# The last expert's context loaded behind the first gathered rows, and a new order of VectorE and ScalarE up to the fourth tile

## The chip, the cores and the metric

The kernel runs on one core of a Trainium2 chip. The time is device time in microseconds, the median of three runs: 295.52 us (295.21 to 295.55).

## The reference

The input x has 4 batches of 512 rows of 512 numbers. Two blocks follow each other, each with a layer norm before and a gated residual after.

```
x = x + tanh(g_xattn) * A(layernorm(x))
x = x + tanh(g_ffn)   * F(layernorm(x))
```

A routes each row by its token id to one of 4 experts: `expert = min(clip(id, 0, 24999) // 6250, 3)`. The expert's three matrices are all the same 512x512 matrix, ctx[e]: `g = silu(h @ ctx[e].T)`, `u = h @ ctx[e].T`, `y = (g * u) @ ctx[e].T`. F averages a batch's rows, picks 2 of 6 experts by a softmax, and mixes `gelu(h @ W1 + b1) @ W2 + b2` of both, with 352 hidden units. All is float32.

## The kernel before

The 2048 rows are sorted by expert into 19 tiles of 128 rows (`TILES`, N/128 + E - 1). The first four tiles are the first tile of each expert, so tile j < 4 uses expert j. The routing is computed on the chip: VectorE ranks the token ids, TensorE inverts the ranking with one-hot matrices (`invert`, L960), and VectorE turns the result into row numbers (`rows_of`, L571), first for the tiles 0 to 3 and later, from `tile_hot`, for the rest. GpSimd gathers the rows of a tile by an indirect DMA (L423) into a ring of six places, and scatters the finished ones (L435).

Float32 products are done in three passes of rounded halves: each operand is split into a high part (ScalarE copies from PSUM with rounding) and a low part (VectorE subtracts the high part from PSUM). For a tile j the steps are: `rows_statistics` and `normalise` (VectorE, with an inverse root on GpSimd between), `transpose_h` (TensorE, L974), `h_high` (ScalarE), `h_low` (VectorE), `first_product` (TensorE, 12 matmuls of 512 columns, L1020), `silu_of` (ScalarE), `up` (VectorE), `transpose_a` (L981), `a_high`, `a_low`, `second_product` (L1034), and `residual` (VectorE, L591).

Before it, each ctx[e] is loaded by one DMA of SP's queue (L347), transposed in four pieces n = 4e to 4e+3 (`transpose_ctx(n)`, L1039) into one of four PSUM banks n mod 4, and split: `ctx_high(n)` on ScalarE (L817), `ctx_low(n)` on VectorE (L625). For the pieces in `BY_ACT` (8 and 9) the low part is made otherwise: TensorE transposes again and subtracts the high part with a negated identity (`rest_of_ctx`, L1051), and ScalarE copies the result (`ctx_low_alone`, L821). A bank is free for piece n + 4 when the low part of piece n is done.

Every engine runs a program in an order written out by hand, and waits on semaphores. SP's queue issues the token ids and the four contexts at once, then waits for much later events. VectorE's order up to the third tile is L630 to L665, ScalarE's L831 to L852, TensorE's L1061 to L1091. After them the tiles are done in loops (L666, L853, L1102), the first block's last tiles overlap the start of the second block, and the four batches of the second block follow.

The change touches the constant `BY_ACT`, the loop of L346, and these three hand-written stretches.

Of the kernel before, what the change touches and what calls it, by code (L numbers as in the profile page):

```python
# [51 lines left out]
class Chain:  # L52
# [18 lines left out]
    def run(self, ins, apart=False):  # L71
        self.wait(self.sign(ins), apart)


def flamingo_kernel(nc, x, ids, ctx, g_xattn, g_ffn, gate_w, w1, b1, w2, b2, out):
# [8 lines left out]
    IDC = N // P  # L84
    FIRST_BY_POOL = 3
    FAR = 1024.0
    WARM = (10, 10)
    TILES = N // P + E - 1
    RING = 6
# [3 lines left out]
    EARLY = TT + E - 1  # L93
    PREP = TILES - 7
    LATER = TILES - E
    BY_ACT = (8, 9)
    BY_DVE = tuple(n for n in range(E * KD) if n not in BY_ACT)
    FC = -(-F2 // P)
    FM = [min(P, F2 - c * P) for c in range(FC)]
# [13 lines left out]
    with ExitStack() as stack:  # L113
# [229 lines left out]
        @block.sync  # L343
        def _(sp):
            sp.dma_start(ids_i[:, :], ids.rearrange("b s -> (b s)").rearrange("(p c) -> p c", c=IDC)).then_inc(ids_here, 16)
            for e in range(E):  # L346
                sp.dma_start(raw_ctx[:, e], ctx[e].rearrange("(k p) d -> p k d", p=P)).then_inc(ctx_here[e], 16)  # L347

            for counted in primed:
                sp.sem_inc(counted, 1)  # L350

            def load_x1(b):
                for t in range(TT):
                    sp.dma_start(x1_of(b, t * DS, DS),
                                 x1_rows[bass.ds(b * S + t * P, P), :]).then_inc(x1_here[t], 16)

            def load_experts(b):
                wait_apart(sp, gate_ready, b + 1, waited)
                full = (FC - 1) * P
                chosen = [sp.value_load(top_idx[0:1, s:s + 1], min_val=0, max_val=NE - 1) for s in range(2)]  # L360
                for s, e in enumerate(chosen):
                    if b > 0:
                        sp.wait_ge(lo_done[s], len(PARTS) * b)
                    raw = w_raw[s]
                    for piece, width in ((0, slice(0, P)), (1, slice(P, F2))):
                        sp.dma_start(part_of(raw, piece),
                                     w1[bass.ds(e, 1), :, width].rearrange("o (k p) f -> p (o k) f", p=P)
                                     ).then_inc((w1_here if width.start == 0 else w1_rest_here)[s], 16)
                    sp.dma_start(raw[:, W1N:W1N + (FC - 1) * D].rearrange("p (c d) -> p c d", d=D),
                                 w2[bass.ds(e, 1), 0:full].rearrange("o (c p) d -> p (o c) d", p=P)).then_inc(w2_here[s], 16)  # L370
                    last = raw[:, W1N + (FC - 1) * D:WN]
                    sp.dma_start(last[0:FM[-1], :], w2[bass.ds(e, 1), full:F2].rearrange("o f d -> (o f) d")).then_inc(w2_here[s], 16)
                    sp.dma_start(last[BIAS_ROW:BIAS_ROW + 1, :], b2[bass.ds(e, 1), :]).then_inc(w2_here[s], 16)

            def store(b):
                for t in range(TT):
                    wait_apart(sp, o_taken, TT * b + t + 2, waited)
                    sp.dma_start(out.rearrange("b s d -> (b s) d")[bass.ds(b * S + t * P, P), :],
                                 x1_of(b, t * DS, D)).then_inc(out_stored, 16)

            sp.wait_ge(ctxT_done, E * KD)
            sp.wait_ge(tiles_landed, EARLY)
            load_x1(0)
            sp.wait_ge(rows_done, 1)
            sp.wait_ge(pads_made, 3)
            load_experts(0)
            sp.wait_ge(tiles_landed, TILES)
            for b in range(0, B - 1):
                wait_apart(sp, h2_ready, TT * b + TT, waited)
                wait_apart(sp, out_stored, 16 * TT * b + 1, waited)  # L390
                load_x1(b + 1)
                load_experts(b + 1)
                store(b)
            store(B - 1)
            wait_primed(sp, out_stored, 16 * TT * B)
# [98 lines left out]
        def _(dve):  # L494
# [89 lines left out]
            def rows_statistics(j):  # L584

                dve.wait_ge(gathered[j % RING], 16 * (j // RING) + 16)
                run(dve.bn_stats(stats1[:, :], ring_row(j, 0, D)), apart=True)  # L587
                run(dve.bn_aggr(mv1[:, :], stats1[:, :]))
                dve.tensor_scalar(ve1[:, :], mv1[:, 1:2], EPS, None, ALU.add).then_inc(ve_ready, 1)
# [11 lines left out]
            def normalise(j):  # L601
                dve.wait_ge(rstd_ready, j + 1)
                at_least(dve, hT_done, j)
                dve.tensor_scalar(h[:, :], ring_row(j, 0, D), mv1[:, 0:1], rstd1[:, :],
                                  ALU.subtract, ALU.mult).then_inc(h_ready, 1)
# [19 lines left out]
            def ctx_low(n):  # L625
                dve.wait_ge(ctx_hi_done, n + 1)
                dve.tensor_tensor(ctx_lo[:, n * F1:(n + 1) * F1], o_ps[n % 4][:, :],  # L627
                                  ctx_hi[:, n * F1:(n + 1) * F1].bitcast(FP32), ALU.subtract).then_inc(ctx_lo_done, 1)

            for n in range(0, 7):  # L630
                ctx_low(n)
            rows_statistics(0)
            ctx_low(7)
            normalise(0)
            rows_statistics(1)
            dve.wait_ge(tg_done, 1)
            h_low(0)
            normalise(1)
# [3 lines left out]
            rows_statistics(2)  # L642
            up(0)
            normalise(2)
            ctx_low(12)
            a_low(0)
            h_low(2)
            up(1)
            dve.wait_ge(ptile_made, 1)
            ones_part = tile_hot[:, :, 1, :]  # L650
            run(dve.tensor_tensor(ones_part, col_h[:, E:TILES].unsqueeze(1).to_broadcast([P, IDC, LATER]),
                                  ptile[:, :].unsqueeze(2).to_broadcast([P, IDC, LATER]), ALU.is_equal))
            dve.tensor_tensor(tile_hot[:, :, 0, :], ones_part, token_h[:, :].unsqueeze(2).to_broadcast([P, IDC, LATER]),
                              ALU.mult).then_inc(tile_hot_done, 1)
            rows_statistics(3)
            ctx_low(13)
            dve.wait_ge(ext_made, 1)
            run(dve.tensor_tensor(ended[:, :, :], col[:, E:TILES].unsqueeze(2).to_broadcast([P, LATER, 2 * E]),
                                  ends[:, :].unsqueeze(1).to_broadcast([P, LATER, 2 * E]), ALU.is_ge))
            run(dve.tensor_reduce(te[:, :], ended[:, :, 0:2 * E - 1], AX_X, ALU.add))  # L660
            dve.scalar_tensor_tensor(te_i[:, :], ended[:, :, E - 1], -float(E), te[:, :], ALU.mult, ALU.add).then_inc(te_made, 1)
            ctx_low(14)
            dve.wait_ge(rows_done, 1)
            rows_of(slice(E, TILES), o_ps[0], LATER, routed)
            ctx_low(15)  # L665
            for j in range(2, PREP):  # L666
                a_low(j - 1)
                normalise(j + 1)
                residual(j - 2)
                h_low(j + 1)  # L670
                up(j)
                rows_statistics(j + 2)
# [117 lines left out]
        def _(sc):  # L790
# [37 lines left out]
            sc.wait_ge(tg_done, 1)  # L828
            bring_tables(ACT.Silu)

            for n in range(0, 8):  # L831
                ctx_high(n)
            sc.wait_ge(gwT_done, 1)
            sc.activation(gwT[:, :, :], y_ps[:, 0:KD * NE].rearrange("p (k e) -> p k e", e=NE), ACT.Copy).then_inc(gwT_copied, 1)
            for c in range(FC):
                sc.activation(b1T[0:FM[c], c, :], y_ps[0:FM[c], (KD + c) * NE:(KD + c + 1) * NE], ACT.Copy).then_inc(gwT_copied, 1)
            ctx_high(8)
            ctx_high(9)
            ctx_low_alone(8)
            ctx_high(10)  # L840
            ctx_low_alone(9)
            ctx_high(11)
            h_high(0)
            ctx_high(12)
            h_high(1)
            silu_of(0)
            ctx_high(13)
            a_high(0)
            h_high(2)
            silu_of(1)  # L850
            ctx_high(14)
            ctx_high(15)  # L852
            for j in range(2, PREP):  # L853
                a_high(j - 1)
                silu_of(j)
# [76 lines left out]
        def _(pe):  # L932
# [130 lines left out]
            transpose_ctx(0)  # L1063
            transpose_ctx(1)
            transpose_ctx(2)
            pe.wait_ge(slot_hot_done, IDC)
            pe.wait_ge(first_hot_done, 1)
            invert(aT_ps, slot_hot, first_hot, E).then_inc(first_rows_done, 1)
            for n in range(3, 8):
                transpose_ctx(n)  # L1070
            turn_small_tables()
            transpose_ctx(8)
            transpose_ctx(9)
            rest_of_ctx(8)
            transpose_ctx(10)
            rest_of_ctx(9)
            transpose_ctx(11)

            transpose_h(0)
            transpose_ctx(12)  # L1080
            first_product(0, 0, lambda: transpose_h(1))
            transpose_ctx(13)
            first_product(1, 1)
            transpose_a(0)
            transpose_h(2)
            transpose_ctx(14)
            second_product(0, 0)
            transpose_ctx(15)
            pe.wait_ge(tile_hot_done, 1)
            pe.wait_ge(ctx_lo_done, by_dve_until(13))  # L1090
# [160 lines left out]
```

## Time and profile before

| | |
|---|---|
| median of three runs | 295.52 us |
| profiled execution, its own time | 295.37 us |
| its span | 293.6 us |
| TensorE (PE) busy | 282.3 us, 96% |
| VectorE (DVE) busy | 205.1 us, 70% |
| ScalarE (ACT) busy | 108.9 us, 37% |
| GpSimd (POOL) busy | 70.1 us, 24% |
| granted TensorE clock, mean | 0.999 of full speed |

The span runs from the first to the last recorded instruction; 1.8 us of the execution's own time lie around it. Busy times are those of single instructions; matmuls are pipelined, so starts of successive instructions tell more than their durations. Names such as L996 are lines of the kernel, often those of a helper that serves many calls.

### The profile page before, as it was taken

To read this page: it belongs to the slowest core of one execution; us is meant where nothing else is said; L and a number is where in the kernel's file an instruction comes from. 1 tells how busy PE (TensorE), PEld (TensorE's weight loads), DVE (VectorE), ACT (ScalarE), POOL (GpSimd) and SP (SyncE) were. 2 spreads that over 40 slices of the span, in tenths; PEclk is the share of its full clock that TensorE was granted. 3 is DMA by queue.
4 is the path that set the end of the run, shared out by engine and by line. 5 is a ranking of instruction groups with operands and counts; after the bars stand their busy time and mean duration, and the time that the engine had idled before them with its cause. 6 is when DMAs were issued, how large, how long until landed. Compare 5 with 4: busy or idle time off the path is not lost.

```text
span 293.6 us, 4400 instructions
## 1 busy us (share of the span) xinstructions
PE 282.3 (96%) x1426; PEld 227.5 (78%) x1426; DVE 205.1 (70%) x449; ACT 108.9 (37%) x191; POOL 70.1 (24%) x108
## 2 busy tenths in 40 slices
PE   6879899999999999999999999999999999999995
PEld 6668688888888888867786877877788777878874
DVE  7867978878887898697769455786465854846133
ACT  4655222222223225444254273335443372442010
POOL 4545245555444554442240000000000000000000
PEclk9999999999999999999999999999999999999999
DMA  6930022232245223169115009640576205730003
GB/s 211 393 118 0 14 96 72 72 111 73 75 143 180 74 72 110 36 187 316 73 44 171 2 6 310 224 143 0 165 231 214 74 0 181 214 145 1 0 0 143
DMA packets 21490, 34.44 MB, mean 117 GB/s; under 512 B 1865, under 2 KB 10063, under 8 KB 21469
## 3 DMA queue, kind: packets, MB, share of 16 engines
q1 hardware_dynamic: 18400, 24.16, 25.3%
q0 software_dynamic: 3040, 9.98, 10.2%
q8 instruction: 12, 0.20, 0.3%
q14 instruction: 10, 0.07, 0.1%
q10 hardware_dynamic: 28, 0.02, 0.0%
HBM read 24.97 MB, written 9.19 MB: 116 GB/s over the span
## 4 chain that ended last, share of the span: by engine, by line
PE 84%; DVE 11%; DMA 2%; issue 1%; ACT 1%; POOL 0%; ACTq 0%; POOLq 0%; DVEq 0%
PE bank L996 31%; PE bank L970 15%; PE bank L971 14%; PE bank L972 14%; PE bank L987 3%; PE bank L978 3%; DMA x_ring<-in_x,get_rows 2%; PE bank L1113 2%; DVE x_odd L730 1%; DVE stats L587 1%; DVE ctx_lo L627 1%; PE bank L936 1%; DVE w_lo L710 1%; DVE w_raw L563 1%; DVE aT_lo L616 1%
## 5 line engine op out<-in xcount | busy, mean ns | idle before, releaser
L970 PE MATMUL bank<-w_lo,ctx_hi 128*128 128x512 f32 (+1 forms) x96 | 38.0, 395 | 0.4 <-DVE ctx_lo L723 0.4
L971 PE MATMUL bank<-w_hi,ctx_hi 128*128 128x512 f32 (+1 forms) x96 | 37.5, 391 | 0.0
L972 PE MATMUL bank<-w_hi,ctx_lo 128*128 128x512 f32 (+1 forms) x96 | 37.4, 390 | 0.0
L710 DVE TENSOR_TENSOR w_lo<-w_raw,w_hi 128x512 fp32r<-128x512 f32 (+2 forms) x24 | 27.6, 1172 | 2.6 <-ACT w_hi L874 2.6
L970 PE MATMUL bank<-ctx_lo,w_hi 128*128 128x512 f32 (+1 forms) x72 | 28.6, 397 | 0.0
L971 PE MATMUL bank<-ctx_hi,w_hi 128*128 128x512 f32 (+1 forms) x72 | 28.2, 392 | 0.0
L972 PE MATMUL bank<-ctx_hi,w_lo 128*128 128x512 f32 (+1 forms) x72 | 28.1, 391 | 0.0
L722 DVE TENSOR_SCALAR ctx_hi<-act,mix 128x512 fp32r<-128x512 f32 x16 | 7.8, 485 | 28.0 <-ACT act L882 28.0
L882 ACT ACTIVATE act<-bank,b1T 128x512 f32<-128x512 f32 x16 | 10.9, 688 | 43.6 <-PE bank L972 42.4
L804 ACT ACTIVATE aT_hi<-bank 128x512 fp32r<-128x512 f32 x18 | 10.8, 599 | 41.0 <-PE bank L987 41.0
L809 ACT ACTIVATE a<-bank 128x512 f32<-128x512 f32 x19 | 11.4, 598 | 37.0 <-PE bank L996 37.0
L874 ACT ACTIVATE w_hi<-w_raw 128x512 fp32r<-128x512 f32 (+2 forms) x24 | 23.4, 1015 | 2.7 <-DMA w_raw<-in_L_ffn_b 2.7
L996 PE MATMUL bank<-ctx_hi,hT_hi 128*128 (+1 forms) x80 | 23.6, 417 | 0.7 <-ACT hT_hi L899 0.5
L970 PEld LDWEIGHTS bank<-w_lo,ctx_hi 128*128 128x128 f32 (+1 forms) x96 | 18.0, 188 | 4.7 <-issue 0.9
L434 POOL TENSOR_TENSOR x_ring<-x_ring,half 128x1 f32<-128x1 f32 x19 | 10.6, 558 | 46.3 <-DVE x_ring L599 46.3
L996 PE MATMUL bank<-ctx_hi,hT_lo 128*128 (+1 forms) x80 | 21.7, 393 | 0.0
L996 PE MATMUL bank<-ctx_lo,hT_hi 128*128 (+1 forms) x80 | 21.6, 392 | 0.0
L996 PE MATMUL bank<-ctx_hi,aT_hi 128*128 (+1 forms) x72 | 21.0, 413 | 0.2
L423 POOL DMA_INDIRECT x_ring<-in_x,get_rows x19 | 19.2, 1012 | 7.7 <-DVE put_rows L576 4.2
L435 POOL DMA_INDIRECT x_scratch<-x_ring,put_rows x19 | 19.7, 1039 | 5.4 <-POOL x_ring L434 5.4
L972 PEld LDWEIGHTS bank<-w_hi,ctx_lo 128*128 128x128 f32 (+1 forms) x96 | 18.0, 188 | 3.8
L971 PEld LDWEIGHTS bank<-w_hi,ctx_hi 128*128 128x128 f32 (+1 forms) x96 | 18.1, 188 | 3.7
(173 smaller groups left out, 559.8 us busy)
## 6 DMA issues: line engine op xcount, KB each, us to landing
raw_ctx<-in_ctx SPq DMA_DIRECT2D x4, 1024.0 KB, 6.8
w_raw<-in_L_ffn_W SPq DMA_DIRECT2D x8, 512.0 KB
w_raw<-in_L_ffn_W SPq DMA_DIRECT2D x8, 448.0 KB, 5.9
x_even<-x_scratch SPq DMA_DIRECT2D x8, 257.0 KB, 3.5
x_odd<-x_scratch SPq DMA_DIRECT2D x8, 257.0 KB, 3.0
w_raw<-in_L_ffn_W SPq DMA_DIRECT2D x8, 256.0 KB, 4.2
out<-x_even SPq DMA_DIRECT2D x8, 256.0 KB, 2.2
out<-x_odd SPq DMA_DIRECT2D x8, 256.0 KB, 2.1
```

The lines of the kernel that those rows point to most:

```text
L423: pool.indirect_dma_start(x_ring[:, r * DS:r * DS + D], None, x_rows, bass.IndirectOffsetOnAxis(get_rows[:, j:j + 1], 0)).then_inc(gathere ...
L434: chain.run(pool.tensor_tensor(deviation, deviation, half[:, 0:1], ALU.pow), apart=True)
L435: pool.indirect_dma_start(x1_rows, bass.IndirectOffsetOnAxis(put_rows[:, j:j + 1], 0), x_ring[:, r * DS:(r + 1) * DS], None).then_inc(scat ...
L710: dve.tensor_tensor(part_of(w_lo[s], piece), part_of(w_raw[s], piece), part_of(w_hi[s], piece).bitcast(FP32), ALU.subtract).then_inc(lo_do ...
L804: sc.activation(aT_hi[:, :, :].rearrange("p k t -> p (k t)"), aT_ps[:, :], ACT.Copy).then_inc(aT_hi_done, 1)
L809: sc.activation(a[:, :], z_bank(j)[:, :], ACT.Silu).then_inc(silu_done, 1)
L874: sc.activation(part_of(w_hi[s], piece), part_of(w_raw[s], piece), ACT.Copy).then_inc(hi_done[s], 1)
L882: sc.activation(dst, hid_ps[k % 2][0:rows, :], ACT.Gelu, bias=b1T[0:rows, c, bass.ds(e, 1)]).then_inc(gelu_done, 1)
L970: pe.matmul(dst, s_hi, m_lo, start=first, stop=False)
L971: pe.matmul(dst, s_hi, m_hi, start=False, stop=False)
L972: return pe.matmul(dst, s_lo, m_hi, start=False, stop=last)
L996: return pe.matmul(dst[:, :], src[:, k, :], weights[:, bass.ds(e * (KD * F1) + k * F1, F1)], start=first, stop=last)
```

## The change

The load of the last expert's context (e = 3) waits on SP until the first gather has landed. The pieces whose low part is made by TensorE and ScalarE are now 0 and 1 instead of 8 and 9. VectorE does pieces 2 to 7 before the first statistics, piece 8 after them and piece 9 after the second statistics; the statistics of tile 3 and the tables for the later tiles come before `a_low(0)`; `normalise(3)` and `residual(0)` are taken out of the loop's first turn and put earlier. TensorE transposes pieces 12 and 13 behind `transpose_h(2)`, and 14 and 15 behind the second product of tile 0.

```diff
+    AFTER_ROWS = E - 1
-    BY_ACT = (8, 9)
+    BY_ACT = (0, 1)
@@ SP
             for e in range(E):
+                if e == AFTER_ROWS:
+                    sp.wait_ge(gathered[0], 16)
                 sp.dma_start(raw_ctx[:, e], ...).then_inc(ctx_here[e], 16)
@@ VectorE
-            for n in range(0, 7):
+            for n in range(2, 8):
                 ctx_low(n)
             rows_statistics(0)
-            ctx_low(7)
+            ctx_low(8)
             normalise(0)
             rows_statistics(1)
+            ctx_low(9)
             dve.wait_ge(tg_done, 1)
             h_low(0)
             normalise(1)
...
             rows_statistics(2)
             up(0)
             normalise(2)
-            ctx_low(12)
+            rows_statistics(3)
+            dve.wait_ge(ptile_made, 1)
+            (tile_hot of L650 to L654, and between its two steps, after
+             dve.wait_ge(ext_made, 1), the comparison `ended` of L658)
             a_low(0)
             h_low(2)
             up(1)
-            (tile_hot; rows_statistics(3); ctx_low(13); ended; te; te_i)
+            normalise(3)
+            ctx_low(12)
+            te
             ctx_low(13)
+            te_i
+            residual(0)
             ctx_low(14)
             dve.wait_ge(rows_done, 1)
             rows_of(slice(E, TILES), o_ps[0], LATER, routed)
             ctx_low(15)
             for j in range(2, PREP):
                 a_low(j - 1)
-                normalise(j + 1)
-                residual(j - 2)
+                if j > 2:
+                    normalise(j + 1)
+                    residual(j - 2)
@@ ScalarE
-            for n in range(0, 8):
+            ctx_high(0)
+            ctx_high(1)
+            ctx_high(2)
+            ctx_low_alone(0)
+            ctx_high(3)
+            ctx_low_alone(1)
+            for n in range(4, 8):
                 ctx_high(n)
             (copies of the small tables)
-            ctx_high(8), ctx_high(9), ctx_low_alone(8), ctx_high(10), ctx_low_alone(9), ctx_high(11)
+            ctx_high(8) ... ctx_high(11)
             h_high(0)
-            ctx_high(12)
             h_high(1)
             silu_of(0)
-            ctx_high(13)
             a_high(0)
             h_high(2)
             silu_of(1)
-            ctx_high(14), ctx_high(15)
+            ctx_high(12) ... ctx_high(15)
@@ TensorE
             transpose_ctx(0), transpose_ctx(1), transpose_ctx(2)
+            rest_of_ctx(0)
             (waits) invert(aT_ps, slot_hot, first_hot, E).then_inc(first_rows_done, 1)
-            for n in range(3, 8):
+            transpose_ctx(3)
+            rest_of_ctx(1)
+            for n in range(4, 8):
                 transpose_ctx(n)
             turn_small_tables()
-            transpose_ctx(8), (9), rest_of_ctx(8), transpose_ctx(10), rest_of_ctx(9), transpose_ctx(11)
+            transpose_ctx(8) ... transpose_ctx(11)
             transpose_h(0)
-            transpose_ctx(12)
             first_product(0, 0, lambda: transpose_h(1))
-            transpose_ctx(13)
             first_product(1, 1)
             transpose_a(0)
             transpose_h(2)
+            transpose_ctx(12)
+            transpose_ctx(13)
+            second_product(0, 0)
             transpose_ctx(14)
-            second_product(0, 0)
             transpose_ctx(15)
```

## Rows read from the trace of the kernel before

**Rows 1.** The page, part 4: shares of the chain that ended last.
```profile
PE 84%; DVE 11%; DMA 2%; issue 1%; ACT 1%; POOL 0%; ACTq 0%; POOLq 0%; DVEq 0%
```

**Rows 2.** The chain in order of time, 0 to 75 us: start, us, what.
```profile
10.49 5.88 DMA x_ring<-in_x,get_rows
...
16.40 0.70 DVE stats L587
...
18.80 0.66 PE bank L978 x4
...
20.14 2.13 PE bank L996 x8
```

**Rows 3.** TensorE's timeline: start, us, instructions, idle time before and its releaser.
```profile
23.48 0.60 PE L1048 MATMUL bank<-ident,raw_ctx 128*128 128x128 f32 x4
23.84 1.18 PE L996 MATMUL bank<-ctx_hi,hT_hi 128*128 128x512 f32 x4
...
26.68 0.60 PE L987 MATMUL bank<-ident,a 128*128 128x128 f32 x4
...
27.97 1.19 PE L996 MATMUL bank<-ctx_hi,aT_hi 128*128 128x512 f32 x4
...
31.66 0.64 PE L987 MATMUL bank<-ident,a 128*128 128x128 f32 x4
...
35.77 0.66 PE L978 MATMUL bank<-ident,h 128*128 128x128 f32 x4 [0.71 <-DVE h L604]
36.52 1.17 PE L996 MATMUL bank<-ctx_hi,aT_hi 128*128 128x512 f32 x4
...
39.36 0.60 PE L987 MATMUL bank<-ident,a 128*128 128x128 f32 x4
...
42.57 0.60 PE L978 MATMUL bank<-ident,h 128*128 128x128 f32 x4
```

**Rows 4.** DMA queues, 0 to 11.5 us: packets, MB, share of 16 engines.
```profile
q1 hardware_dynamic: 1721, 3.15, 79.8%
```

**Rows 5.** DMA queues, 13.5 to 14.0 us (q1 is SP's, q0 the gathers').
```profile
q1 hardware_dynamic: 92, 0.18, 100.4%
q0 software_dynamic: 2, 0.01, 4.3%
```

**Rows 6.** DMA queues, 14.5 to 15.0 us.
```profile
q0 software_dynamic: 56, 0.18, 98.4%
```

**Rows 7.** Instructions on x_ring, 34 to 36 us: the fifth gather, and its landing.
```profile
L423 POOL DMA_INDIRECT x_ring<-in_x,get_rows x1: 1089/1089/1089, 34.3 to 34.3; - x1
...
DMA to landing us min/median/max: 3.5/3.5/3.5
```

**Rows 8.** The same, 13 to 14 us: the third gather's landing.
```profile
DMA to landing us min/median/max: 5.0/5.0/5.0
```

**Rows 9.** TensorE's timeline: invert, and the first rest_of_ctx up to the next transpose.
```profile
8.98 0.54 PE L962 MATMUL bank<-w_raw 128*128 128x8 f16 x16 [0.53 <-DVE w_raw L565]
...
15.08 0.66 PE L1056 MATMUL bank<-ident,raw_ctx 128*128 128x128 f32 x4 [0.25 <-issue]
...
15.81 0.60 PE L1048 MATMUL bank<-ident,raw_ctx 128*128 128x128 f32 x4
```

**Rows 10.** ScalarE's timeline: the first three high copies.
```profile
7.68 1.57 ACT L819 ACTIVATE ctx_hi<-bank 128x512 fp32r<-128x512 f32 x3 [0.57 <-PE bank L1048]
```

**Rows 11.** VectorE's timeline: the first seven low parts; the first residual up to h_low(3).
```profile
10.11 4.27 DVE L627 TENSOR_TENSOR ctx_lo<-bank,ctx_hi 128x512 fp32r<-128x512 f32 x7
...
35.63 0.74 DVE L595 SCALAR_TENSOR_TENSOR x_ring<-bank,tg,x_ring 128x512 f32<-128x512 f32 x1
...
37.43 0.68 DVE L610 TENSOR_TENSOR hT_lo<-bank,hT_hi 128x512 fp32r<-128x512 f32 x1
```

**Rows 12.** Instructions on raw_ctx, 0 to 40 us: the contexts' loads.
```profile
DMA to landing us min/median/max: 5.7/6.8/8.0
```

**Rows 13.** Busy time by stretch, 17 to 18 us: PE, PEld, DVE, ACT, POOL, then PEclk, DMA share, GB/s.
```profile
17.00:18.00 1.00, 0.07 (x1) 0.00 (x0) 0.93 (x4) 0.81 (x2) 0.42 (x1) 1.00 0.35 139
```

More of the change, by code:

```diff
@@ L644, in _ @@
             normalise(2)
-            ctx_low(12)
+            rows_statistics(3)
+            dve.wait_ge(ptile_made, 1)
+            ones_part = tile_hot[:, :, 1, :]
+            tiled = chain.sign(dve.tensor_tensor(ones_part, col_h[:, E:TILES].unsqueeze(1).to_broadcast([P, IDC, LATER]),
+                                                 ptile[:, :].unsqueeze(2).to_broadcast([P, IDC, LATER]), ALU.is_equal))
+            dve.wait_ge(ext_made, 1)
+            ended_by = chain.sign(dve.tensor_tensor(ended[:, :, :], col[:, E:TILES].unsqueeze(2).to_broadcast([P, LATER, 2 * E]),
+                                                    ends[:, :].unsqueeze(1).to_broadcast([P, LATER, 2 * E]), ALU.is_ge))
+            chain.wait(tiled)
+            dve.tensor_tensor(tile_hot[:, :, 0, :], ones_part, token_h[:, :].unsqueeze(2).to_broadcast([P, IDC, LATER]),
+                              ALU.mult).then_inc(tile_hot_done, 1)
             a_low(0)
@@ L648, in _ @@
             up(1)
[L649 to L655, printed above, removed]
+            normalise(3)
+            ctx_low(12)
+            chain.wait(ended_by)
+            ended_by = chain.sign(dve.tensor_reduce(te[:, :], ended[:, :, 0:2 * E - 1], AX_X, ALU.add))
             ctx_low(13)
[L657 to L660, printed above, removed]
+            chain.wait(ended_by)
             dve.scalar_tensor_tensor(te_i[:, :], ended[:, :, E - 1], -float(E), te[:, :], ALU.mult, ALU.add).then_inc(te_made, 1)
+            residual(0)
             ctx_low(14)
@@ L836, in _ @@
                 sc.activation(b1T[0:FM[c], c, :], y_ps[0:FM[c], (KD + c) * NE:(KD + c + 1) * NE], ACT.Copy).then_inc(gwT_copied, 1)
[L837 to L842, printed above, removed]
+            for n in range(8, 12):
+                ctx_high(n)
             h_high(0)
-            ctx_high(12)
             h_high(1)
             silu_of(0)
-            ctx_high(13)
             a_high(0)
@@ L850, in _ @@
             silu_of(1)
-            ctx_high(14)
-            ctx_high(15)
+            for n in range(12, 16):
+                ctx_high(n)
             for j in range(2, PREP):
@@ L1068, in _ @@
             invert(aT_ps, slot_hot, first_hot, E).then_inc(first_rows_done, 1)
-            for n in range(3, 8):
+            transpose_ctx(3)
+            rest_of_ctx(1)
+            for n in range(4, 8):
                 transpose_ctx(n)
             turn_small_tables()
[L1072 to L1077, printed above, removed]
+            for n in range(8, 12):
+                transpose_ctx(n)
             transpose_h(0)
-            transpose_ctx(12)
             first_product(0, 0, lambda: transpose_h(1))
-            transpose_ctx(13)
             first_product(1, 1)
```

## The prediction

> **What bounds the kernel now.** The page's shares of the chain that ended last come first: TensorE holds 84% of it, VectorE 11%, DMA 2% [rows 1]. So time is to be had only where TensorE waits or does work that it can be spared. The chain in order of time over the first 75 us shows where the DMA share sits: one gather, 5.88 us from its issue at 10.49, landing at 16.37, and behind it the statistics at 16.40, the transpose of the normalised rows at 18.80 and the first product at 20.14 [rows 2]. From landing to first product is a fixed string of small steps, 20.14 - 16.37 = 3.77 us, or 3.74 us from the start of the statistics. TensorE's timeline shows the next visible wait, 0.71 us before `transpose_h(3)` at 35.77, released by VectorE's h; from 36.52 on it goes from tile to tile without one, 3.21 us from `transpose_a` to `transpose_h` (39.36 to 42.57) [rows 3]. From there to the end nothing is touched and nothing is tied to an absolute time, so I carry the shift of `transpose_a(2)`, at 39.36 now, to the end one to one.
>
> Why did the gather take 5.88 us? The DMA rows say it: by 11.5 us SP's queue had moved 3.15 MB, which is three contexts of 1.05 MB [rows 4]. From 13.5 to 14.0 it still moved 92 packets, and the gathers' queue two [rows 5]; from 14.5 to 15.0 the gathers' queue had 56, at 98.4% of the engines [rows 6]. The gather of 34.35, on a quiet queue, landed in 3.5 us [rows 7]. So the fourth context, 2.7 us of transfer at 0.19 MB per half microsecond, stands in front of the rows.
>
> The Trainium skill ("DMA: Bandwidth & Descriptors", section "Queues, rings and completion order") says that each DMA engine goes round-robin between the queues that have work, packet by packet; by that rule the gathers would have taken a share of the engines from their first descriptor, and the fourth context would cost them at most a doubling, not a standstill. The rows of 13.5 to 14.0, 92 packets against 2, speak against it, unless the gather's descriptors came late; what that would make of the time is the first rival.
>
> **The change part by part.**
>
> *Fourth context behind the first rows.* With three contexts gone at 11.5 us, the gather meets an empty queue. Its price is bounded by the quiet 3.5 us [rows 7] and by the 5.0 us of the third gather, which had others before it [rows 8]. I take 3.5, since it has the same size and nothing beside it but the next gather's 1.3 us later.
>
> *First two contexts' low halves by TensorE and ScalarE instead of numbers 8 and 9.* One `rest_of_ctx` costs TensorE 0.73 us (15.08 to 15.81) [rows 9]. The first now stands before the `invert` which gives the first rows. The three transposes end their issue at about 8.3, ScalarE's first copy ends at 8.28 (three copies in 1.57 from 7.68, each 0.60) [rows 10], so the rest goes 8.33 to 9.06; `invert` starts at 8.98 now [rows 9], thus 0.1 us later. Gather issued at 10.59, landing at 14.1 (at 5.0: 15.6).
>
> *VectorE before the rows.* It now does numbers 2 to 7 ahead of the statistics; the seven of before took 4.27 us, 0.61 each, from 10.11 [rows 11]. But number 5 must wait for a bank: second rest done 10.74, ScalarE's low copy 10.77 to 11.37, transpose 5 to 12.06, its high copy to 12.70, then numbers 5, 6, 7 at 0.61 each: 12.75 to 14.58. So the statistics start at max(14.1, 14.58) = 14.58 (with the slow gather 15.6) and the first product at 14.58 + 3.74 = 18.32, against 20.14: 1.8 us gained. What is late next is VectorE itself, by 0.5 us. Numbers 8 to 11 have all four banks free again: TensorE's four transposes and ScalarE's copies end by 16.3, before `h_high(0)` at 17.7. In the old order transposes 11 and 12 waited behind VectorE's number 7, which stood behind the statistics; now it stands ahead, at no cost.
>
> *TensorE from first product to `transpose_a(2)`.* Before, 39.36 - 20.14 = 19.22 us. Its parts, from the timeline's starts [rows 3]: transpose 12 was hidden in the wait at 19.29; now it comes on the busy line, +0.36 (as transpose 13: 23.48 to 23.84). Transposes 13, 14, 15 only move. The wait at `transpose_h(3)` was 0.71 us after the end of the last product, and 0.16 more if counted from where the next instruction could have started (0.87), and the transpose after a wait took 0.75 to the next start instead of 0.36. Both vanish if h(3) is ready. New: 19.22 + 0.36 - 0.87 - 0.39 = 18.32 us, so `transpose_a(2)` is at 36.64, 2.7 us earlier.
>
> Is h(3) ready? TensorE would ask for it 2.84 + 0.36 us before 36.64, at 33.4. On VectorE, normalise(2) comes 1.8 us earlier, at 24.0; then the fourth tile's statistics (1.1 us) and the three table steps (0.33, 0.20, 0.41) end at 26.45 (`ptile` of GpSimd, also 1.8 earlier, is there at 25.3); `a_low(0)`, `h_low(2)`, `up(1)` at 0.6 each to 28.3, normalise(3) to 28.7. Ready 4.7 us ahead. The later tiles' `invert` needs ctx_low(12), at 29.35; TensorE comes to it 0.4 us before `transpose_a(1)`, which is at 36.64 - (39.36 - 31.66 - 0.87 - 0.39) = 30.2, so at 29.8: 0.45 us of cover. `residual(0)` takes 1.8 us (35.63 to 37.43) [rows 11] and now stands before the routing of the later tiles: it goes 30.3 to 32.1, rows 5 and on are known at 33.3, the fifth gather is issued at 33.6 (34.35 now) and lands at 37.1. Its statistics then run 1.1 us to 38.2, the inverse root 0.6, normalise to 39.45; `transpose_h(4)` is due at 36.64 + 3.21 = 39.85. Cover 0.4 us; so this part of the gain is thin but kept. The second residual frees y at 40.1, and the product that needs it starts at 40.2.
>
> *The fourth context's arrival.* SP issues it at 14.1. The landings that the trace has of the contexts took 5.7 to 8.0 us from their issue, on queues that filled up [rows 12]: 19.8 to 22.1. TensorE asks for it after two first products and two of the three transposes that stand between 26.68 and 27.97: 18.32 + (23.48 - 20.14) + (26.68 - 23.84) + 0.86 = 25.4. With the slow gather both sides move, 23.6 against 26.4. Hidden by at least 2.8 us. The gathers behind it: the second is issued at 12.1 and should land at 15.6, before the context's first byte; third and fourth are needed only at 22 and 24. SP has nothing else queued behind its wait but the priming of semaphores used after 110 us.
>
> Sum: 1.8 + 0.9 = 2.7 us off the profiled execution's 295.37 us (span 293.6): 292.7. The median of the runs is 295.52, 0.15 above it; I take 292.8 for the time.
>
> **Rivals.**
>
> *The rows come no sooner* (20%). For it: descriptors of the first gather may be slow in the making; its instruction took 1.19 us against the 1.09 of rows 7, and no row shows a gather at 10 us with a free queue. Against: 34.35's 3.5 us. Then landing at 16.47, first product 20.2, and only the 0.9 us of TensorE's line less 0.1 is left: 294.6. Between it and the forecast lies the 5.0 us landing: gain 0.8 + 0.9, 293.7.
>
> *A new wait at the fourth tile or before* (10%). The covers of 0.45, 0.4 and 0.1 us are small against a working with errors of 0.2 a step. If the fifth gather takes 5.0 us instead of 3.5, `transpose_h(4)` waits 1.1 us: 293.9.
>
> *Slower: the clock falls in the new gap* (5%). TensorE's transposes end at 15.3 and the rows' transpose comes at 17.0, then 0.7 us more of waiting. At 17 to 18 us of before it was busy 0.07 and the granted clock stayed 1.00 [rows 13]; the new gap is 1.7 us, half as long again as that 1.08. Should it fall from 2.4 to 1.2 GHz there, each 4 products of 0.92 us take 1.84, half of the time at the low clock is lost; from 5.4 us at that level on, the change is slower; at 8 us it loses 4.0 and the kernel ends at 296.7.
>
> *It does not do what it says* (3%): some order leaves TensorE's line as it was, 295.4.
>
> **Numbers.** The forecast has 62%: 292.1 to 293.4. With the 5.0 us landing, the thin covers and the late rows it reaches to 294.7, which leaves out the slower case and no change. Under 292.1 would need a landing and a VectorE both 0.5 us earlier than worked out. What a measurement can tell from no change is 0.2%, 0.6 us. All cases but the last two are faster by more: 0.89; within: 0.05; slower: 0.06.
>
> **What would show it.** Right: gather 10.6 to landing near 14.1; no packets of SP's queue from about 12.5 to 15.5; statistics at 14.6; first product at 18.3; no wait at `transpose_h(3)`, `transpose_a(2)` at 36.6, and the same spacing after. Wrong: the gathers' first packets still at 14 with an empty queue; a wait on raw_ctx before transpose 12; a wait before `transpose_h(4)`; a granted clock under 1.00 after 17 us.

## The result and the profile after

The changed kernel takes 293.29 us (median of four, 292.63 to 293.42) against 295.53 (295.21 to 295.68): a ratio of 0.9921, 95% interval 0.9904 to 0.9938. Its profiled execution took 292.63 us, span 290.8, and is the fastest of the four; forecast was 292.7 for the profiled one and 292.8 for the median.

The chain in order of time of the changed kernel (start, us, what), to be held against [rows 2]:

```profile
5.41 1.59 PE bank L946 x10
7.00 1.34 PE bank L1058 x12
8.34 0.54 PE bank L1066 x4
8.87 0.23 PE bank L1068
9.10 0.45 PE bank L972 x16
...
10.51 1.19 POOL x_ring L426
...
15.70 0.58 POOL rstd L431
...
16.91 0.67 PE bank L988 x4
...
18.25 2.12 PE bank L1006 x8
...
36.76 0.44 PE bank L997 x4
...
39.95 0.44 PE bank L988 x4
```

The 5.88 us of DMA have left the chain. TensorE's transposes of context 0 (L1058) and the rest (L1066, L1068) now lead into the invert (L972), and GpSimd's instructions stand where the DMA stood: it issues the four gathers one after the other and makes the first tile's inverse root (L431) behind them, at 15.70. The ten transposes of L946 multiply the identity into a bank that nobody reads; they keep TensorE busy ahead of context 0's transposes. TensorE's timeline, against [rows 3]:

```profile
16.91 0.66 PE L988 MATMUL bank<-ident,h 128*128 128x128 f32 x4 [1.58 <-DVE h L607]
18.25 1.19 PE L1006 MATMUL bank<-ctx_hi,hT_hi 128*128 128x512 f32 x4 [0.69 <-ACT hT_hi L809]
...
33.39 0.60 PE L988 MATMUL bank<-ident,h 128*128 128x128 f32 x4
...
36.60 0.60 PE L997 MATMUL bank<-ident,a 128*128 128x128 f32 x4
...
39.80 0.60 PE L988 MATMUL bank<-ident,h 128*128 128x128 f32 x4
```

The wait of 0.71 us before `transpose_h(3)` is gone (33.39 carries no idle time), `transpose_a(2)` starts at 36.60 instead of 39.36, and the spacing behind it is as before (3.20 us, 36.60 to 39.80). VectorE's timeline, against [rows 11]:

```profile
10.12 1.28 DVE L630 TENSOR_TENSOR ctx_lo<-bank,ctx_hi 128x512 fp32r<-128x512 f32 x2
11.86 0.69 DVE L630 TENSOR_TENSOR ctx_lo<-bank,ctx_hi 128x512 fp32r<-128x512 f32 x1 [0.47 <-ACT ctx_hi L829]
12.72 1.89 DVE L630 TENSOR_TENSOR ctx_lo<-bank,ctx_hi 128x512 fp32r<-128x512 f32 x3 [0.17 <-ACT ctx_hi L829]
14.52 0.68 DVE L590 BATCH_NORM_STATS2 stats<-x_ring 128x6 f32<-128x512 f32 x1
```

The statistics follow number 7 with no idle time: the rows were there. SP issued the fourth context at 14.1, which is when the first gather had landed. The second gather, issued at 12.00, came only at about 17.3: VectorE waited 0.44 us for it before the second statistics at 17.29. What the queues moved from 18 to 19 us (packets, MB, share) shows the price of the load's new place:

```profile
q1 hardware_dynamic: 180, 0.37, 100.5%
q0 software_dynamic: 2, 0.00, 1.1%
```

The third and fourth gather, issued at 13.26 and 14.52, landed 5.6 and 8.0 us after their issue; they had taken 5.0 and 4.4 before.

### The profile page after: what moved, and what is told of

Its sections match the earlier page's. It is cut to its first block, busy times and chain, and to the rows that moved or that the text cites. A ratio compares the mean times of both kernels' runs of the same rounds, so it can differ in the third digit from the quotient of the medians.

```text
span 290.8 us, 4400 instructions
## 1 busy us (share of the span) xinstructions
PE 280.8 (97%) x1426; PEld 227.6 (78%) x1426; DVE 205.3 (71%) x449; ACT 108.8 (37%) x191; POOL 70.5 (24%) x108
## 4 chain that ended last, share of the span: by engine, by line
PE 88%; DVE 7%; POOL 2%; issue 1%; ACT 1%; ACTq 0%; POOLq 0%; DVEq 0%
PE bank L1006 33%; PE bank L980 15%; PE bank L981 14%; PE bank L982 14%; PE bank L997 3%; PE bank L988 3%; PE bank L1122 2%; POOL x_ring L426 1%; PE bank L946 1%; PE bank L1058 1%; DVE x_odd L740 1%; DVE w_lo L720 1%; PE bank L1131 1%; DVE ctx_lo L733 1%; DVE hT_lo L613 0%
## 5 line engine op out<-in xcount | busy, mean ns | idle before, releaser
L1006 PE MATMUL bank<-ctx_hi,hT_hi 128*128 (+1 forms) x80 | 23.5, 415 | 1.1 <-ACT hT_hi L809 0.7
```

The lines of the kernel that those rows point to most:

```text
L1006: return pe.matmul(dst[:, :], src[:, k, :], weights[:, bass.ds(e * (KD * F1) + k * F1, F1)], start=first, stop=last)
```

## The experiments

All times are medians; each set has its own runs of the kernel before beside it (295.27 to 295.44).

**The changed kernel once more.**

> The changed kernel itself, once more. Theory A (the second gather lands late, behind the fourth context, and its cover is thin): in the profile of the changed kernel h(1) was ready 0.16 us before TensorE asked for it, so the executions spread between 292.6 and 293.4, median about 293.2, and a profile of a longer one shows a wait before transpose_h(1) at about 20 us. Rival B (the spread comes from later, the weight loads of the second block): the prologue is the same to 0.1 us in any profile, transpose_a(2) at 36.6, and the extra 0.7 us lies behind 120 us. Rival C (a shift of the whole set by the chip): median near 292.7.

293.25 us (292.66 to 293.66), ratio 0.9926 (0.9913 to 0.9939). The profiled execution was one of 293.25, and its chain says where its 0.62 us more came from:

```profile
5.40 2.22 PE bank L946 x10
7.62 1.31 PE bank L1058 x12
8.93 0.53 PE bank L1066 x4
9.46 0.23 PE bank L1068
9.69 0.40 PE bank L972 x16
```

The first context was transposed from 7.62 instead of 7.00, and from there all is shifted: `transpose_h(0)` 17.46, `transpose_a(2)` 37.21 (+0.61). Theories A and B and rival C all fall: TensorE had no idle time before `transpose_h(1)` at 20.77, next to nothing was added behind `transpose_a(2)`, and the median is not 292.7. Five profiles with this order of the front and the late load have these starts of transpose 0 and of `transpose_h(0)`: 7.00, 16.91; 7.19, 17.03; 7.26, 17.10; 7.54, 17.39; 7.62, 17.46.

What delayed transpose 0 was not its load. Context 0 landed 5.2 to 6.0 us after its issue at 1.2 in all the profiles of this case, thus by 7.2 at the latest, and only the kernel before shows a wait for it (0.20 us). The late starts follow the ten transposes of the identity ahead of it: from 5.33 they took 1.66 us in the changed kernel's first profile and 2.29 in this one (1.59 and 2.22 in the chains), between 1.64 and 2.40 in all profiles. The kernel whose context 0 came earliest (5.2 us, low halves of 8 and 9, below) has the full 2.40. The first ten took 2.4 us in every profile, where twelve transposes of context 0 take 1.5, so TensorE begins at about half its later pace and speeds up at a time that differs from execution to execution. The rows give a granted clock of 1.00 there; what sets that time stays open.

**The fourth context loaded at once.**

> The changed kernel with the fourth context loaded at once, as before; all orders as changed. My step: the first gather lands at about 16.4 again, the statistics start there, first product 20.1, only TensorE's line is shorter by 0.8 to 0.9: transpose_a(2) at 38.5, 294.6 us. Rival (the rows come no sooner, the gather's own making is the bound, and the gain was the order alone): landing stays near 14.1 and the time near 293.2.

```diff
-                if e == AFTER_ROWS:
-                    sp.wait_ge(gathered[0], 16)
```

296.02 us (295.60 to 297.50), 1.0033 (1.0019 to 1.0046): slower than the kernel before, where 294.6 was expected. The statistics start at 16.37 after a wait for the DMA and the first product at 20.11, as expected; so the rival that the rows come no sooner is out. But TensorE idled 2.73 us before `transpose_h(0)`, and by the busy times by stretch (PE, PEld, DVE, ACT, POOL, PEclk, DMA, GB/s) its granted clock fell to half, 1.2 GHz. The mean clock of all eleven executions is 0.988 to 0.994; the three at 0.988 took 297.1 to 297.5.

```profile
18.00:20.00 2.00, 0.66 (x4) 0.42 (x4) 1.83 (x6) 0.54 (x1) 0.33 (x2) 1.00 0.12 47
20.00:22.00 2.00, 1.89 (x6) 1.52 (x7) 2.00 (x5) 0.05 (x1) 1.66 (x6) 0.72 0.00 0
22.00:24.00 2.00, 2.00 (x9) 1.60 (x8) 0.56 (x1) 0.00 (x0) 1.50 (x6) 0.50 0.00 0
24.00:26.00 2.00, 2.00 (x10) 1.64 (x10) 1.19 (x2) 1.20 (x2) 0.71 (x2) 0.93 0.00 0
```

**The late load alone, orders as before.**

> The kernel before with the late load of the fourth context alone, orders as before. Theory: the first rows land at 14.1, but transpose 12 stands on TensorE between transpose_h(0) and the first product, and the fourth context lands only 8 us after its issue at 14.1, at 22.1; the first product starts at about 22.8 to 23.0 instead of 20.14, and the kernel is slower than before by 2 to 2.8 us: 297.5 to 298.3. Rival (the load lands in 5.7 us on a free queue): first product at 20.5, about 295.5.

```diff
             for e in range(E):
+                if e == E - 1:
+                    sp.wait_ge(gathered[0], 16)
```

300.24 us (300.02 to 300.43), 1.0165 (1.0152 to 1.0178). The rows landed at 14.06, and transpose 12 waited for the context, which came 8.0 us after its issue at 14.1; behind the wait TensorE ran at 1.2 GHz until about 28 us:

```profile
22.08 1.11 PE L1050 MATMUL bank<-ident,raw_ctx 128*128 128x128 f32 x4 [4.13 <-DMA raw_ctx<-in_ctx]
```

```profile
22.00:24.00 2.00, 1.92 (x7) 1.73 (x8) 0.00 (x0) 0.60 (x1) 0.51 (x2) 0.50 0.00 0
24.00:26.00 2.00, 2.00 (x7) 1.52 (x6) 0.00 (x0) 0.00 (x0) 0.00 (x0) 0.50 0.00 0
```

Of the 4.9 us lost, 2.7 are the late first product (22.84 against 20.14), as the theory had it; the other 2.2 fall in the stretch at the low clock. In this profile transpose 0 started at 7.71, later than in any of the five above, and the invert all the same at 9.02 (8.98 before): in the old order it does not wait for the copy of context 0.

**The fourth context behind the second gather, and behind the fourth.**

> The changed kernel with the fourth context behind the second gather's landing instead of the first's. Theory A: the second gather lands at 15.6 to 16 instead of 17.3, the second statistics do not wait, h(1) has 0.6 us of cover instead of 0.16, and the executions stay near 292.6 with a spread under 0.3 us. The context lands at 23 to 23.8, before TensorE asks at 25.3. Rival B: no change of the median, 293.2.

> The changed kernel with the fourth context behind the landing of the fourth gather. That gather is issued at 14.5 to 15.1 and lands at about 18.3 when nothing else moves; the context is issued then. If its landing takes 5.7 us on a free queue, it is there at 24.0 and the time is 293.2 as for the first gather; if it takes 8 us, transpose 12 waits from 25.3 to 26.3 and the time is 294.2.

Behind the second: 293.01 us (292.70 to 293.62), 0.9925 (0.9913 to 0.9938). The second statistics no longer wait and the third and fourth gathers land in 3.9 and 3.6 us, but the spread is that of the changed kernel: theory A falls once more. Behind the fourth: 292.65 us (292.57 to 293.20), 0.9911 (0.9896 to 0.9927). The context is issued at 18.4 and lands in 5.1 us, at 23.5, and TensorE does not wait for it. Its profile had transpose 0 at 7.19; the ranges of the executions overlap, so I call neither better than the first place.

**rest_of_ctx(0) behind the invert.**

> The changed kernel with rest_of_ctx(0) behind the invert of the first rows instead of ahead of it. In three profiles the first context's transposes began at 7.5 to 7.8 us instead of 7.0, and the invert, now behind the rest, at 9.6 to 9.8 instead of 9.0, so both the gather and VectorE's string began 0.5 to 0.6 later. Theory D (two strings end together at the statistics: the gather, and the banks' string context 0, rests, transposes, VectorE to its number 7): here the gather goes out at 10.5 and lands at 14.1 whatever the first context does, but VectorE comes to the statistics only at about 15.1; no gain, 293.2 to 293.4. Rival E (the gather alone is last): statistics at 14.2 to 14.5, 292.6.

```diff
-            rest_of_ctx(0)
             invert(aT_ps, slot_hot, first_hot, E).then_inc(first_rows_done, 1)
+            rest_of_ctx(0)
```

294.94 us (293.66 to 295.24), 0.9978 (0.9963 to 0.9993). The invert went at 8.99 and the statistics started only at 15.18, behind number 7 without idle time, though the first rows had landed by 14.1: theory D holds, E falls. This profile had an early transpose 0 (6.82 in TensorE's timeline, 6.84 in the changed kernel's), so the move cost 0.66 us against 14.52: the rest of piece 0 now started at 9.39 instead of 8.22, and the banks came free later. What neither theory had: in four of six executions (294.8 to 295.2; mean clock 0.992 to 0.994) the clock fell, the other two took 293.66 and 293.92 at 1.00. In the profile, with the first product at 18.91:

```profile
16.00:18.00 2.00, 0.43 (x4) 0.42 (x4) 1.87 (x5) 1.57 (x3) 0.57 (x1) 1.00 0.85 246
18.00:20.00 2.00, 1.31 (x7) 0.96 (x5) 1.93 (x6) 0.60 (x1) 1.23 (x4) 0.93 0.96 349
20.00:22.00 2.00, 2.00 (x6) 1.43 (x6) 1.37 (x3) 0.00 (x0) 1.53 (x6) 0.50 0.33 129
```

**The load at once, with the wait filled.**

> The kernel of the load at once, with 20 transposes of the identity into an unused bank on TensorE in the wait before transpose_h(0), where it stood idle for 2.7 us and its clock fell from 2.4 to 1.2 GHz at about 20.6 us. Theory F (the whole of what that kernel lost against my 294.6 is the clock): granted clock 1.00 throughout, first product at 20.1 as there, 294.6 us. Rival G (the fall of the clock is a by-product, and the loss lies in the order): 296 us at a clock of 1.00.

```diff
+            pe.wait_ge(gwT_copied, 1 + FC)
+            for _ in range(20):
+                pe.transpose(y_ps[:, 0:P], ident[:, :], ident[:, :])
             transpose_h(0)
```

295.42 us (294.28 to 295.59), 0.9993 (0.9980 to 1.0006). The clock stayed at 1.00 throughout the prologue and the first product at 20.06. Three of the five executions have 2.9 us outside their span instead of the 1.8 of all others, for which I have no cause; by spans it is 292.5 to 292.9 (median 292.6) against 293.8 to 295.7 (294.2) without the transposes. So some 1.6 us of that kernel's loss are the clock (`transpose_a(2)` comes at 38.42 against 39.97), and with the usual 1.8 outside it would be at 294.3 to 294.7, the 294.6 of theory F.

**VectorE's old order from the third tile on.**

> The changed kernel with VectorE's order behind normalise(2) as before: a_low(0), h_low(2), up(1), then the tables, statistics of the fourth tile, the last context's low halves, and normalise(3) and residual(0) in the loop. My step: TensorE then waits at transpose_h(3) again, 0.5 us and 0.4 of unpipelined start, so transpose_a(2) comes 0.9 us later than in the changed kernel: 294.1 us. Rival (VectorE has caught up by then, since the first tiles came sooner): 293.3.

294.46 us (293.91 to 296.21), 0.9979 (0.9961 to 0.9996), about 1.2 above the changed kernel's median; by the profile alone the way from the first product to `transpose_a(2)` is 37.83 - 18.44 = 19.39 us, against 36.60 - 18.25 = 18.35. Of the difference 0.27 us lies at the second invert (1.14 us behind the start of transposes 14 and 15, against 0.87), and 0.8 at `transpose_h(3)`, which came 0.39 later behind the last products and took 0.75 to the next start instead of 0.35:

```profile
34.25 0.66 PE L982 MATMUL bank<-ident,h 128*128 128x128 f32 x4 [0.23 <-DVE h L607]
```

One execution of six (296.21, mean clock 0.994) had the lower clock.

**Low halves of 8 and 9 instead of 0 and 1.**

> The changed kernel with the low halves of pieces 8 and 9 made by TensorE and ScalarE, as before, instead of 0 and 1, so that nothing stands ahead of the invert; late load and the rest as changed. VectorE then does 0 to 7 ahead of the statistics: 10.1 + 8 x 0.61 = 15.0, against 14.5 to 15.1 in the changed kernel, whatever the first context does. Theory D: first product at 18.8 to 18.9, 293.3 to 293.5 us with a spread under 0.4, so that this part of the change gained nothing in most executions. Rival (my sum's step): 0.45 us slower than the changed kernel's median, 293.7.

293.45 us (293.29 to 293.70), 0.9937 (0.9923 to 0.9950). Statistics at 15.08, first product at 18.93. The spread is 0.4, and the median only 0.2 above the changed kernel's: exchanging the pieces earns 0.7 us against the changed kernel's fastest profile (18.93 - 18.25) and 0.1 against its slow one (18.80). This profile has the slowest front of all: transpose 0 at 7.52 in the timeline, the three transposes in 1.82 us instead of 1.50, and the invert at 9.17. So an order with nothing but the transposes ahead of the invert is not quite safe either; it loses 0.2 us where the changed kernel lost 0.5 to 0.7.

**Towards a better version.**

> A version meant to be better: rest_of_ctx(0) behind the invert; VectorE takes the first statistics after its number 5 and does 6 to 11 between the later steps; transpose 11 and its high copy stand behind transpose_h(0), in the wait for its copy; the fourth context waits for the second gather. Theory D: the gather at 10.5, landing at 14.1, is now the only string that ends at the statistics, at 14.1; first product at 17.9 (18.25 to 18.8 in the changed kernel), independent of the first context's landing; 292.3 to 292.6 us with a spread under 0.4. If VectorE falls behind by the second or third tile instead, 293.0 or more.

```diff
-                    sp.wait_ge(gathered[0], 16)
+                    sp.wait_ge(gathered[1], 16)
@@ VectorE
-            for n in range(2, 8):
+            for n in range(2, 6):
                 ctx_low(n)
             rows_statistics(0)
-            ctx_low(8)
+            ctx_low(6)
             normalise(0)
+            ctx_low(7)
             rows_statistics(1)
-            ctx_low(9)
+            ctx_low(8)
...
@@ TensorE (and rest_of_ctx(0) behind the invert)
+            transpose_ctx(8), (9), (10)
             transpose_h(0)
+            transpose_ctx(11)
```

292.55 us (292.53 to 292.57), 0.9907 (0.9894 to 0.9920). Transpose 0 started at 7.73 in this profile, the invert at 9.06, the statistics at 14.15, and TensorE had its longest wait before the first product cut from 1.58 to 0.78 us:

```profile
15.90 0.66 PE L1061 MATMUL bank<-ident,raw_ctx 128*128 128x128 f32 x4 [0.78 <-issue]
16.71 0.66 PE L991 MATMUL bank<-ident,h 128*128 128x128 f32 x4 [0.15 <-DVE h L607]
17.31 0.66 PE L1061 MATMUL bank<-ident,raw_ctx 128*128 128x128 f32 x4
18.05 1.20 PE L1009 MATMUL bank<-ctx_hi,hT_hi 128*128 128x512 f32 x4
```

> The better version once more. The invert stands ahead of everything that waits for the first context, and TensorE has work in the wait for the rows. Theory: 292.5 to 292.7 us again, with a spread well under the 0.8 us of the changed kernel, the mean granted clock 0.997 to 1.00 in every execution. If the narrow spread was chance: executions up to 293.3.

292.92 us (292.64 to 293.33), 0.9913 (0.9899 to 0.9927): the narrow spread was chance. The ten transposes of the identity took 2.40 us in the first profile and 1.75 in this one:

```profile
5.33 2.40 PE L949 MATMUL bank<-ident 128*128 128x128 f32 x10
```

```profile
5.33 1.75 PE L949 MATMUL bank<-ident 128*128 128x128 f32 x10
```

Transpose 0 so started at 7.52 and at 6.92 by the timeline, and yet the prologue is the same (invert 8.99 and 8.98, first product 18.05 in both, `transpose_a(2)` 36.54 and 36.56). With nothing that waits for a copy ahead of the invert, and nothing behind number 5 ahead of the statistics, a slow front no longer reaches the rows. Against the changed kernel's fastest profile (36.60) little is gained; by the profiles the gain is in the executions with a slow front (37.21 against 36.54). The profiled execution loses 0.37 us at the 13th tile, where statistics waited for a gather while SP's queue was loading the second block's first rows:

```profile
88.47 0.70 DVE L590 BATCH_NORM_STATS2 stats<-x_ring 128x6 f32<-128x512 f32 x1 [1.22 <-DMA x_ring<-in_x,get_rows]
```

> The better version with GpSimd's inverse root of the first tile ahead of its fourth gather, that of the third tile one step earlier, and VectorE's piece 11 behind normalise(2): the 0.26 us that normalise(0) waited for GpSimd go, first product at 17.8, 292.3 us. If VectorE is the bound by the third tile, 292.55 as without it.

292.80 us (292.47 to 292.95), 0.9913 (0.9898 to 0.9928). GpSimd is the third string here: in `e9` the inverse root stood behind the fourth gather's instruction, at 15.48, and `normalise(0)` waited 0.26 us. Without that the first product is at 17.86 and `transpose_a(2)` at 36.38, both 0.2 earlier, but there is no gain in the median: it can't be told from the version before it. The median over both sets of `e9`'s executions, 292.64, is 0.6 under that of the changed kernel's nine, 293.25, over different sets.

## Why the prediction was right, and which term was mis-sized

- **Load behind the rows.** Right. Landing at 14.1 (14.1 forecast) and, without this edit, at 16.35. The kernel with the load at once puts its worth at 2.7 us: 1.3 to 1.9 by position (18.80 and 18.25 against 20.11; 1.8 forecast), the rest, which the sum had not, by a clock that falls without it in the new order.
- **The rows come no sooner** (20%): refuted. The gather that met the fourth context landed at 16.37 and 16.35 whether issued at 10.49 or at 11.22, in both cases some 2 us after the context was nearly through (6 packets of SP's queue from 14.5 to 15.0). That the queues were served in turn, packet by packet, as the Trainium skill has it ("DMA: Bandwidth & Descriptors", section "Queues, rings and completion order"), is not what these rows show: 92 packets against 2 before [rows 5], 180 against 2 from 18 to 19 us of the changed kernel. In other stretches the queues do share: 35 packets against 31 from 16 to 17 us. What decides between the two is open.
- **rest_of_ctx(0) ahead of the invert.** The mis-sized term. I priced it at 0.1 us from one trace, in which the ten transposes of the identity ahead of context 0's were the fastest of all profiles (1.64 us). In other executions these take up to 2.40, transpose 0 starts up to 0.7 later, and then the copy that the rest needs holds the invert back: 9.46 to 9.69 in three profiles, 0.5 to 0.7 later than before instead of 0.1. The order of before lost nothing in one slow front (7.71 and still 9.02) and 0.2 in the slowest. Of nine executions of the changed kernel seven are 0.4 to 1.0 us above the fastest; the profiled one of them has its 0.6 us from here. That the other six, and with them the 0.5 us between the forecast and the median, have it from here too is likely but not shown: even the order that is safe from it spreads by 0.8. The profiled execution, 292.63 against 292.7, met the forecast because its front was fast, which is luck.
- **VectorE last at the statistics, at 14.58:** right, 14.52. With the invert moved alone VectorE still came last, at 15.18, with the rows there at 14.1.
- **TensorE's line 0.9 us shorter:** right (19.22 to 18.35); undone by VectorE's old order alone (19.39).
- **Thin covers at the fourth tile:** held; `transpose_h(4)` at 39.80, 39.85 forecast. The fifth gather was issued at 33.49 (33.6).
- **The shift carried to the end one to one:** right. From `transpose_a(2)` to the end of the span it is 254.2 us before and after (293.6 - 39.36, 290.8 - 36.60), and 254.1 to 254.4 in eleven other profiles; only `e15`, with its wait at the 13th tile, has 254.5.
- **The fourth context hidden:** right, with the 22.1 us that I had as the late end. Wrong was that the second gather would land at 15.6, before the context's first byte: it came at about 17.3, and the fourth took 8.0 us. Both stayed hidden: with the context behind the second gather, where VectorE does not wait, the median is 293.01, inside the changed kernel's range.
- **The clock** (5%): it did not fall in the nine executions of the changed kernel (mean 0.997 to 0.999), but I had the danger too small: the kernel with the invert first, whose `transpose_h(0)` is 0.1 us behind that of the changed kernel's later profile, lost 1.0 to 1.5 us by it in four of six executions, and the one with VectorE's old order, 0.2 behind the earlier profile, 1.9 in one of six.
- **The chances:** the cases with a faster kernel add up to 92% (62, 20 and 10), where the last line gives 0.89.

## What to carry to other kernels

Before a step is put ahead of the chain's head, ask what it waits for in its worst execution, not in the one profiled: a step that costs 0.1 us by its length can pass on all the jitter of the work in front of it. Look up what that work is: here the load was the obvious suspect, and the rows cleared it. Once a wait is shortened, other strings may end close behind it (here VectorE's 0.4 us behind the rows, and GpSimd's next), so look at all of them before moving one. And when TensorE's idle time is made or moved, read the granted clock of the next microseconds in the profile and the mean clock of each execution, since a prologue can be a tenth of a microsecond away from half speed.

## What the runs showed of the hardware

- With a wait of 1.58 us before `transpose_h(0)` and 0.69 after it, the clock stayed at 2.4 GHz in the changed kernel. In the kernel with the invert first, whose waits have the same lengths (1.57 and 0.69), it fell to 1.2 for some 3.4 us in the profiled execution, and by the mean clock in three of the five others. The length of a wait alone does not decide; what else does was not settled. In the kernels with waits of 2.73 and 4.13 us in their profiles the mean clock was down (0.986 to 0.994) in every execution.
- At 1.2 GHz four products lasted 1.91 us, and 1.71 to the next start, where they take 1.08 and 0.93 at 2.4. The kernel with the load at once was at the low level for about 3.4 us (an estimate from the PEclk column, 20 to 26 us) and lost 1.55 by it up to `transpose_a(2)`.
- TensorE's first twenty transposes of the identity did not run at one pace: the first ten took 2.4 us in every profile, the second ten 1.64 to 2.40, with a granted clock of 1.00 in the rows.
- A context of 1 MB landed 7.7 to 8.6 us after its issue with three gathers under way or still to be issued, 6.0 to 7.7 with two, and 5.1 with none.
